# Pairwise products of a field-interaction layer: 128 B of unused memory in front of all on-chip buffers

## What is computed

```python
i_idx, j_idx = jnp.triu_indices(f, k=1)
xw = jnp.einsum('bfe,ed->bfd', x, W)
return xw[:, i_idx, :] * x[:, j_idx, :]      # (2048, 496, 64), float32
```

## Time and profile before

| | |
|---|---|
| median of 3 runs | 655.48 us (654.12 to 655.57) |
| the profiled execution, own time | 655.77 us |
| its span, first to last instruction | 654.0 us |
| VectorE busy | 568.9 us, 87% of the span |
| TensorE busy | 209.3 us, 32% |
| ScalarE busy | 101.8 us, 16% |
| moved by DMA | 277.00 MB, 424 GB/s over the span |
| share of the 16 DMA engines' time, stores and loads | 92.4% and 6.2% |

### The profile page before, as it was taken

One profiled execution on the slowest core, in us unless ns is written; L12 is line 12 of the kernel. 1 busy time (PEld: TensorE's weight loads), 2 busy tenths in 40 slices (PEclk: granted clock), 3 DMA queues, 4 the chain that ended last, 5 costly groups with the idle time before them and its releaser, 6 DMA issues.

```text
span 654.0 us, 3858 instructions
## 1 busy us (share of the span) xinstructions
PE 209.3 (32%) x1280; PEld 157.5 (24%) x1280; DVE 568.9 (87%) x528; ACT 101.8 (16%) x385; POOL 0.7 (0%) x6
## 2 busy tenths in 40 slices
PE   5946080803407043070430704316080431400000
PEld 4734060602305032050330603214060321300000
DVE  3999999899689996899968999999999999999940
ACT  3412030302103021030210302112030211200000
POOL 0000000000000000000000000000000000000000
DMA  8999999999999999999999999999999999999994
GB/s 329 433 450 417 447 417 415 451 418 428 434 424 438 429 433 418 432 437 430 437 416 432 430 440 426 442 421 446 424 443 427 438 423 442 426 437 433 427 443 211
DMA packets 8524, 277.00 MB, mean 424 GB/s; under 512 B 1088, under 2 KB 1088, under 8 KB 1088
## 3 DMA queue, kind: packets, MB, share of 16 engines
q1 hardware_dynamic: 6912, 260.05, 92.4%
q10 hardware_dynamic: 1600, 16.81, 6.2%
HBM read 16.81 MB, written 260.05 MB: 423 GB/s over the span
## 4 chain that ended last, share of the span: by engine, by line
DMA 54%; DVE 39%; issue 2%; PE 0%; ACTq 0%; DVEq 0%; ACT 0%
DMA out_dram<-out_ring 54%; DVE out_ring L198 39%; DMA x_sb<-in_x_dram 1%; ACTq L164 0%; PE xw_bank L125 0%; PE xT_ps L115 0%; DVEq L55 0%; ACT xw_sb L160 0%; DVEq L197 0%
## 5 line engine op out<-in xcount | busy, mean ns | idle before, releaser
L198 DVE TENSOR_TENSOR out_ring<-xw_sb,x_sb 128x384 f32<-128x384 f32 (+9 forms) x528 | 568.9, 1155 | 59.5 <-DMA out_dram<-out_ring 48.2
L125 PE MATMUL xw_bank<-W_sb,xT_sb 64*128 64x64 f32 x1024 | 138.9, 429 | 347.1 <-ACT xT_sb L155 345.1
L125 PEld LDWEIGHTS xw_bank<-W_sb,xT_sb 64*128 64x128 f32 x1024 | 118.1, 320 | 385.6 <-issue 358.9
L155 ACT COPY xT_sb<-xT_ps 128x256 f32<-128x256 f32 x128 | 48.1, 376 | 383.0 <-DVE out_ring L198 339.1
L115 PE MATMUL xT_ps<-identity,x_sb 128*128 128x128 f32 x256 | 83.7, 442 | 7.4 <-DMA x_sb<-in_x_dram 7.4
L160 ACT COPY xw_sb<-xw_bank 128x128 f32<-128x128 f32 x256 | 55.6, 270 | 74.3 <-PE xw_bank L125 74.3
L115 PEld LDWEIGHTS xT_ps<-identity,x_sb 128*128 128x128 f32 x256 | 39.4, 208 | 20.4 <-DMA x_sb<-in_x_dram 7.4
L155 ACT ACT_TABLE_LOAD x1 | 1.3, 1283 | 5.1 <-issue 5.1
L93 POOL TENSOR_SCALAR_AFFINE_SELECT identity<-identity 128x128 f32<-128x128 f32 x1 | 0.3, 295 | 0.2 <-POOL identity L91 0.2
L91 POOL MEMSET identity<- 128x128 f32 x1 | 0.2, 205 | 0.3 <-POOLq L211 0.3
L211 POOL MEMSET const-bfloat16-1.0<- 128x1 bf16 x1 | 0.1, 103 | 0.0
## 6 DMA issues: line engine op xcount, KB each, us to landing
out_dram<-out_ring SPq DMA_DIRECT2D x32, 5280.0 KB, 26.5
out_dram<-out_ring SPq DMA_DIRECT2D x16, 5312.0 KB, 25.6
x_sb<-in_x_dram ACTq DMA_DIRECT2D x6, 2048.0 KB, 21.5
x_sb<-in_x_dram ACTq DMA_DIRECT2D x4, 1024.0 KB, 13.9
W_sb<-in_W_dram ACTq DMA_DIRECT2D x2, 16.0 KB, 2.0
```

Of the source, the lines that this page charges most:

```text
L125: last = nc.tensor.matmul(xw_ps[g % 2][odd][:, m, :], xT_sb[g % 2][rows, m, :], W_sb[rows, :], start=True, stop=True)
L155: nc.scalar.copy(xT_sb[g % 2][:], xT_ps[g % 2][:]).then_inc(xT_copied, 1)
L198: last = nc.vector.tensor_tensor(slot[:, place:place + n, :], xw_sb[t % 2][:, i:i + 1, :].to_broadcast([LANES, n, E]), x_sb[buf][:, r, j:j ...
```

## The change

One more SBUF tensor, `skew`, is allocated ahead of all others where the first free address, rounded up to 32, is no multiple of 256. Here it has 32 elements, 128 B per partition. No instruction reads or writes it. `x_sb0` then starts at 16,640 = 65 x 256 in place of 16,512, and each of the thirteen buffers lies 128 B further up, at a multiple of 256. All addresses relative to one another stay as they were, as do the HBM side of every DMA, and every engine's instructions and their order; the lines behind the change are numbered 5 higher.

```diff
@@ -13,6 +13,7 @@
 CUTS = (0, 165, 330, 496)
 CHUNKS = len(CUTS) - 1
 XW_PRIME = 4
+ALIGN = 256
 
 
 def pair_pieces(F):
@@ -62,6 +63,10 @@
         def sem(name):
             return ctx.enter_context(nc.semaphore(name))
 
+
+        skew = -(-nc.sbuf_base // 32) * 32 % ALIGN
+        if skew:
+            sb("skew", [LANES, (ALIGN - skew) // 4])
         x_sb = [sb(f"x_sb{n}", [LANES, ROWS, F, E]) for n in range(XBUFS)]
         xw_sb = [sb(f"xw_sb{n}", [LANES, F, E]) for n in range(2)]
         out_ring = [sb(f"out_ring{n}", [LANES, SLOT * E]) for n in range(CHUNKS)]
```

## The result

| | before | changed |
|---|---|---|
| median | 655.43 us (654.12 to 655.91, 22 runs) | 654.21 us (654.03 to 654.94, 22 runs) |
| mean of these runs | 655.09 us | 654.24 us |
| runs above 655.0 us | 13 of 22 | 0 of 22 |
| span of the profiled execution | 654.0 us | 652.5 us |

The ratio is 0.9988, with a 95% interval of 0.9982 to 0.9993: the changed kernel is faster by some 0.8 us, 0.4 to 1.2. That is less than the 2 us that I had taken for what can be told from no change, but with 22 runs each it is clear of noise. The spread says as much as the median. These 22 runs of the kernel before lie at 654.1 to 654.8 or at 655.4 to 655.9 us; those of the changed kernel all but one at 654.0 to 654.5. The profiled execution of before, 655.77 us, was one of the upper group, so the two profiles differ by 1.5 us of span, more than the kernels do on average.

A forecast was written before the change was run, and what follows sets the result against it. The prediction took the DMA engines' time per row of bytes as the bound. All terms were taken as 0, so 655.77 + 0 = 655.77 us profiled, less 0.29 us to the median: 655.5 us, range 652.9 to 656.8.

The forecast's parts named there:

- What bounds the kernel: Whole kernel: the DMA engines' time per row of bytes; queues 98.6% full, the slowest engine sets each landing and the end.
- Stores: the cost of a row's odd start: Stores' reads of SBUF: 0 to 4.8 ns per row, up to 1.8 us per engine; the lower end, nothing, was taken.
- The 1.8 us: Stores: upper end if 128 B of each row are fetched in vain, 4.8 ns on 384 rows per engine.
- Loads of x: Loads' SBUF side moves: 0.4 us at most, taken as 0; the remaining 0.9 us per loaded tile called a queue collision.
- VectorE, ScalarE, TensorE, the start: Compute engines and the first loads: operands keep their distances, a few rows cost a few ns; all taken as 0.
- the signs named for "right": Late tile 38.0 to 38.1 us, 434 GB/s, landings 25.6 and 26.5 us, store share 92.4%, VectorE 568.9 us unchanged.
- (a): Stores: the fetch in vain is real, 1.8 us cheaper, 2.2 if loads gain too: 653.7 or 653.3 us; 15%.
- (b): End of kernel: the slowest engine, 8.0 us behind, catches up by 4 to 8 us: 648 to 652 us; 5%.
- (c): Store landings: engines ask in step and the slowest falls further behind; 659.5 us with half as much lag again; 8%.
- (d): Whole change does nothing, as when the offset were not what was thought; the forecast's case, no chance of its own.

## Why the prediction was wrong

The forecast was 655.5 us and no change; measured were 654.21 us, inside the range, and a change that is clear of noise, which I had given 15% only from 2 us on. What moved the time was a small thing, and the step that failed is a small one.

*What bounds the kernel* was right: the DMA engines, and of them the slowest. VectorE's idle time on stores went from 48.2 to 46.6 us, and its wait for ScalarE stayed at 10.3. (The 98.6% belong to the store queue and the load queue together; the text has two store queue rows.)

*Stores: the cost of a row's odd start taken as nothing.* Right for a row by itself: the commonest time is the same, late tiles are 38.02 to 38.09 us, and without the later loads the distance is 0.09 us. The 1.8 us, 4.8 ns on each of 384 rows, do not show. What I had left out is that an odd start can cost nothing alone and something in company. I had priced it as a sum over rows, the same in each; the runs show a cost of time that comes only in some tiles.

By the page "DMA: Bandwidth & Descriptors" of the Trainium skill, in "How a descriptor splits into AXI transactions", the odd start costs each such row 4 beats of 32 B; on the SBUF side of these stores no such steady cost shows, neither at 128 B past a block nor at 4 B past a multiple of 32. The page's unit of 256 B agrees with the runs, since 64 or 256 B of shift gave nothing, and 128 B did.

*Loads of x: the step that failed.* The term for a collision of stores and loads was put at 0. I saw that a tile with a load takes 5.7 us more where its bytes make 4.8, called the remaining 0.9 us "a collision of two queues, which a start address has no obvious hand in", and took 0. The changed kernel's tiles take 42.8 us, 4.8 more: the 0.9 us are gone. The term was on the page of my own argument, in us, and worth up to 3 x 0.9 = 2.7 us, since the fourth of the later loads comes before the stores set the pace; the tiles of before scatter (43.8, 43.7, 43.1), and some of the loss is made up in the tile behind (37.4 us once, and after every load in the trace with aligned load buffers). 1.47 us were left of it in the two traces, and 0.7 to 0.85 us on average. I also looked at the wrong side of the loads: it is the stores' reads, not the loads' writes.

*VectorE, ScalarE, TensorE, the start* at 0: right, busy times unchanged.

*The signs.* All but one of the signs named for "right" came true: late tiles of 38.0 to 38.1 us, landings of 26.5 and 25.6 us, a share of 92.4% and VectorE's 568.9 us; from 480 to 600 us the rate was 433 in place of 434 GB/s. The kernel got faster all the same, because these signs look at the late tiles, where no load moves, at medians, which three longer landings do not shift, and at a share of a span that shrinks along. The sign that would have shown it is the tile with a load.

*The rivals.* (a) is refuted as a mechanism, though the changed kernel's store share, 0.924 x 652.5 = 602.9 us (603.0 by the packet records), looks like its forecast of 602.5. The shares alone would have seemed to confirm it; the pair without loads, as fast with either start, and the commonest row told them apart. (b) and (c) are refuted: the lag at the end is 7.9 us against 8.0. (d) is refuted by the kernel with aligned store buffers, which shows that the offset is what counts.

*What stays open:* why the store rows with odd starts stretch beside a load, why beside the loads up to 340 us and not beside the added ones behind 400 us, and why they stretch late in the kernel too. The runs show when and by how much, not what the engines wait for. That the loads are the cause, and not the time at which they move, rests on the pair without later loads. Nor was it tried why one DMA engine lags. In four late tiles of the changed kernel (394 to 546 us) 11 or 12 rows of a tile's 384 take at least 12 ns longer, 0.6 to 0.9 us in all. A tile at the slowest engine's pace takes 38.1 - 37.45 = 0.6 us more than one at the average pace. By this estimate these rows could all be that one engine's, but the records do not name it.

## What to carry to other kernels

Where stores fill the DMA engines and loads share them, it is worth a try to start the buffers that are stored at a multiple of 256 B per partition: it costs less than 256 B of each partition, gave 0.1% here, and made all runs but one agree within 0.4 us in place of 1.8. A remainder that a known cost doesn't explain (here 0.9 us in each tile with a load) is where a change with no price of its own can act: give it a case, not a zero. To test a cost that is said to sit in each row, take away what the rows meet. To test one in meetings, change their number and nothing else, and then look where in the chain the distance arises: here the times of more loads looked like proof, and the traces showed that the added ones cost nothing more.

## What was not expected of the hardware

A row with an odd start is not slower by itself: commonly 1561 ns for 42,240 B at a multiple of 256 B, 128 B past one and 4 B past a multiple of 32 alike. With odd starts 482 of 4096 rows were longer by 1 to 11 ns, 1500 in the kernel without later loads and 108 in the one with two more; with aligned ones 63 to 75. And lengthened rows need not cost time: in the pair without loads the average row is 3.3 ns longer and the kernel 0.09 us, since one engine, 6 us behind the next at the end in both kernels, sets the pace.
